# A third fixed order of the steps, with its lags and PSUM banks, for a delta-rule attention, softmax attention and mixture-of-experts kernel on one core

## The reference

```
x = x + delta_rule_block(layernorm(x))
x = x + transformer_block(layernorm(x))

delta_rule_block:   q, k, v = silu(causal_conv4(x @ Wq / Wk / Wv)), 16 heads of 64; rope(q), rope(k), both normalised
                    beta = sigmoid(x @ bw + bb);  alpha = exp(-exp(A_log) * softplus(x @ gkw + gkb + dt_bias))
                    per token: o = q S + D (q.k) v;  S = alpha (S - beta k (k S)) + beta k v
                    ((x @ Wg) * silu(rmsnorm(o) * onorm_w)) @ Wo
transformer_block:  x + softmax attention (16 heads of 8) on layernorm(x); then a router picks 2 of 8 experts;
                    each expert is gelu(m @ W1[e] + b1[e]) @ W2[e] + b2[e], with 512 hidden features
```

## Time and profile before

| | us |
|---|---|
| median of three runs | 5545.79 |
| lowest and highest run | 5541.89, 5554.14 |
| the profiled execution | 5533.59 |
| its span, first to last instruction | 5531.7 |

### The profile page before, as it was taken

One profiled execution on the slowest core, in us unless ns is written; L12 is line 12 of the kernel. 1 busy time (PEld: TensorE's weight loads), 2 busy tenths in 40 slices (PEclk: granted clock), 3 DMA queues, 4 the chain that ended last, 5 costly groups with the idle time before them and its releaser, 6 DMA issues.

```text
span 5531.7 us, 111231 instructions
## 1 busy us (share of the span) xinstructions
PE 4792.2 (87%) x40448; PEld 3609.5 (65%) x40448; DVE 4623.1 (84%) x11457; ACT 3445.0 (62%) x6166; POOL 2085.5 (38%) x1485
## 2 busy tenths in 40 slices
...
GB/s 59 10 11 34 43 43 34 28 32 37 43 43 34 24 32 41 43 33 32 33 33 42 43 33 32 32 34 43 43 34 32 32 34 43 43 34 32 31 34 56
DMA packets 214453, 197.13 MB, mean 36 GB/s; under 512 B 13848, under 2 KB 176416, under 8 KB 209696
## 3 DMA queue, kind: packets, MB, share of 16 engines
...
## 4 chain that ended last, share of the span: by engine, by line
DVE 52%; PE 38%; issue 8%; ACT 1%; SPq 0%; DMA 0%; POOL 0%; DVEq 0%; POOLq 0%; ACTq 0%
PE bank L984 36%; DVE acc L1390 10%; DVE tmpb L1556 6%; DVE NP L1526 6%; DVE Gam L1559 5%; DVE mx L1653 3%; DVE Gam L1512 3%; DVE moe L1738 2%; PE bank L988 2%; DVE QK L1671 1%; DVE QK L1479 1%; DVE Gam L1563 1%; DVE rot L1475 1%; DVE ms L1603 1%; DVE Kt L1543 1%
## 5 line engine op out<-in xcount | busy, mean ns | idle before, releaser
L1390 DVE SCALAR_TENSOR_TENSOR acc<-bank,conv_w,acc 128x255 f32<-128x255 f32 (+2 forms) x2304 | 925.1, 470 | 27.3 <-ACT acc L791 26.4
L717 POOL TENSOR_TENSOR sq<-acc 128x256 f32<-128x256 f32 x256 | 191.2, 747 | 1734.5 <-ACT acc L797 1722.3
L984 PE MATMUL bank<-QK 64*128 64x256 f32 (+1 forms) x4096 | 603.3, 352 | 211.8 <-DVE mx L1653 97.7
L984 PE MATMUL bank<-W,h 128*128 128x128 f32 x4096 | 579.7, 302 | 190.1 <-issue 103.3
L984 PEld LDWEIGHTS bank<-W,h 128*128 128x128 f32 x4096 | 551.7, 215 | 237.1 <-issue 129.6
L984 PE MATMUL bank<-mT,W 128*128 128x256 f32 x2048 | 626.4, 447 | 60.3 <-issue 39.7
L984 PEld LDWEIGHTS bank<-QK 64*128 64x128 f32 (+1 forms) x4096 | 288.6, 142 | 523.7 <-issue 346.0
L966 ACT ACTIVATE h<-bank,b 128x256 f32<-128x256 f32 x1024 | 416.7, 479 | 288.6 <-PE bank L984 286.7
L984 PEld LDWEIGHTS bank<-mT,W 128*128 128x128 f32 x2048 | 420.9, 220 | 219.2 <-issue 155.3
L729 POOL TENSOR_TENSOR rot<-rot,sin 128x512 f32<-128x512 f32 x256 | 337.3, 1317 | 450.8 <-DVE rot L1475 450.8
L1559 DVE TENSOR_TENSOR Gam<-Gam,tmpb 128x31 f32<-128x31 f32 (+15 forms) x992 | 448.1, 452 | 34.1
...
## 6 DMA issues: line engine op xcount, KB each, us to landing
W<-in_W SPq DMA_DIRECT2D x512, 256.0 KB, 3.2
...
```

What stands on the lines that cost most here:

```text
L984: return mm(out_, lhsT, rhs, start=first, stop=last)
L1390: v.scalar_tensor_tensor(acc[:, n % 2, m, j:T], ps[:, m, 0:T - j], conv_w[:, kind, c, PAD - j:KT - j], acc[:, n % 2, m, j:T], ALU.mult, AL ...
```

## The change

All five lists and the bank table are replaced; no step function is changed, and every list holds the same set of steps. Some steps change sides of the point at which a turn is cut, and their lags follow: the lists of the engines begin some nine steps earlier in the cycle, SyncE's largest lag is 4, not 3, so `turns` runs one turn more, in which only SyncE has steps left. Two lines of each table:

```diff
     "sp": """
-        xnG:0@1 x1:0@3 expert:1@3 expert:0@3 expert:2@3 expert:3@3 expert:4@3 expert:5@3 QK1:0@1 store:0@3 expert:7@3
-        expert:6@3 xin:0@0""",
+        expert:6@4 expert:7@4 store:0@4 xnG:0@1 expert:0@3 x1:0@3 expert:1@3 QK1:0@1 expert:2@3 expert:3@3 expert:4@3
+        xin:0@0 expert:5@3""",
...
 BANK = """
-    GT:0=2 KS:0=2 KS:1=6 QS:0=1 QS:1=0 S:0=6 Wo:0=3 alpha:0=0 alpha:1=1 alpha:2=5 alpha:3=7 alpha:4=4 alpha:5=7
+    GT:0=7 KS:0=6 KS:1=3 QS:0=6 QS:1=7 S:0=6 Wo:0=6 alpha:0=3 alpha:1=0 alpha:2=7 alpha:3=5 alpha:4=1 alpha:5=6
```

More of the change, by code:

```diff
@@ L57 @@
[L57 to L58 removed]
+        Dv:1@2 dots:6@1 cos:6@1 QSadd:0@2 QSadd:1@2 dots:7@1 root:0@2 sin:6@1 norm:0@2 rstd:0@0 cos:7@1 root:1@2
+        norm:1@2 sin:7@1 nrm:0@1 frstd:0@2 frstd:1@2 X:0@1 cos:0@0 dots:0@0 sin:0@0 cos:1@0 dots:1@0 sin:1@0 cos:2@0
+        dots:2@0 dots:3@0 vscale:0@1 vscale:1@1 sin:2@0 cos:3@0 sin:3@0 cos:4@0 dots:4@0 sin:4@0 Dv:0@1 dots:5@0 cos:5@0
@@ L59 @@
+        frstd:2@2 sin:5@0 R1:0@1 R1:1@1 xs:0@2""",
     "act": """
[L60 to L68, removed]
@@ L69 @@
-        silu:7@0 low:2@1 square:6@0 ex:0@2 low:3@1 gelu:0@2 gelu:1@2 square:7@0""",
-    "pe": """
[L71 to L77, removed]
-        max:12@2 max:11@2 max:14@2 max:15@2 up:14@3 up:13@3 up:15@3 mrow:1@2 mrow:0@2 mrow:2@2 sums:0@0 st:0@2 down:6@3
-        st:3@2 st:2@2 st:1@2 down:7@3 pv:0@2 st:4@2 mrow:3@2 st:5@2 st:6@2 st:7@2 qk:3@0 st:8@2 st:11@2 st:9@2 pv:1@2
-        st:10@2 st:12@2 sums:1@0 st:13@2 pv:2@2 st:14@2 qk:4@0 sums:2@0 st:15@2 qk:6@0 qk:5@0 pv:3@2 join1:0@1 sums:3@0
-        join1:1@1 ctx:0@2 join2:0@1 join2:1@1 ctx:1@2 top:0@1 ctxT:0@2 top:1@1 cross:0@1 fWo:0@2 cross:1@1 low:0@1
-        sums:4@0 low:1@1 qk:7@0 S:0@1 o:1@1 KS:0@1 KS:1@1 QS:0@1 o:0@1 top:2@1 sums:5@0 top:3@1 cross:2@1 mT:0@2
-        cross:3@1 router:0@2 low:2@1 QS:1@1 low:3@1 up:1@2 up:0@2 o:2@1 o:3@1 alpha:1@0""",
```

77 lines of the change are left out of this document (49 added, 28 removed).

## The result

The changed kernel takes 5247.2 us (median of four runs, 5244.47 to 5256.83). The kernel before took 5543.84 us on the same chip (5531.1 to 5554.14). The ratio is 0.9469, 95% interval 0.9446 to 0.9493: 5.3% faster. I had forecast 5610 us, slower, with 5455 us as the lower end of the range. The sign was wrong and the range did not hold the time.

A forecast was written before the change was run, and what follows sets the result against it. A turn is a TensorE-bound stretch (some 50 us) plus a VectorE-bound one (some 117 us). 4.2-1.9-0.2 = +2.1 us a turn, times 31 = +65 us; 5533.6+65+12 = 5610 us, range 5455 to 5700.

The forecast's parts named there:

- T: The start of `join1:0` on TensorE, right behind `close`, from which the prediction counts times within a turn.
- A: The stretch from T to `o:3`, bound by TensorE: +4.2 us a turn, ends +1.9 and +6.7.
- both `join2` 3.6: TensorE behind `close`: both `join2` matmuls take 3.6 us, so they end at T+12.5.
- my first rival: TensorE's clock comes back earlier, at T+6: -2.9 us a turn in all, 5456 us; chance 0.17.
- The tap wait: VectorE behind `close`: L1390 waits some 7 us a turn for ScalarE's `tap:5`.
- B: VectorE's `solve` steps beside GpSimd: -1.9 us a turn, ends -6.4 and +1.
- come just before `close`: Both `vscale` on GpSimd run among the last short `solve` steps, costing twice 1.7 us a turn.
- my second rival: The ports are free: `vscale` falls wholly beside the transposes, -2.0 us a turn in all, 5484 us; chance 0.20.
- the burst beside maxima: GpSimd's burst runs beside VectorE's `max` reductions, which read PSUM, giving back all 6.4 us a turn.
- the price of a meeting: A `vscale` on GpSimd blocks one `solve` step on VectorE, taken as 1.7 us each.
- C: Other waits and gaps, with 1 us saved and 0.8 for `max:0`: -0.2 us a turn, ends -2 and +2.
- The table load of `ex`: ScalarE: `ex` with its table load (1.28 us) stands before the copy of `top:3`, for which `cross:3` waits.

The follow-up runs named there:

- a_qk6_late: The changed kernel with `qk:6` moved from between `ctx:0` and `ctx:1` to behind `cross:1` on TensorE: 5334.6 us, ratio 0.9641.
- b_region: The kernel before with `ctx:0`, `qk:6`, `ctx:1` behind `join1:0` (`ctx:1` in bank 3) and ScalarE's `upper:0` ahead of `join1:0`: 5551.2 us, ratio 1.0031.
- a_tap5: The changed kernel with ScalarE's `tap:5` moved ahead of the `join2` copies: 5234.2 us, ratio 0.9462.
- a_vscale_early: The changed kernel with `vscale:0` and `vscale:1` moved ahead of `dots:3` on GpSimd: 5379.8 us, ratio 0.9729.
- a_swap1_late: The changed kernel with VectorE's `swap:1` moved from behind `max:10` to behind `solve:12`: 5392.5 us, ratio 0.9761.
- b_vscale_late: The kernel before with `vscale:0` and `vscale:1` moved behind `dots:3` on GpSimd: 5515.0 us, ratio 0.9969.
- b_ctx_qk6b: The kernel before with `ctx:0`, `qk:6`, `ctx:1` moved behind `join1:0` on TensorE, VectorE's `ctx` steps matched, `ctx:1` in bank 3: 5556.7 us, ratio 1.0041.

## Why the prediction was wrong

**What bounds a turn: right.** A stretch from T to `o:3` bound by TensorE and one bound by VectorE; in the turns shown both became shorter, by 2.6 to 6.3 us (T+49.1 and T+52.8 became T+46.5) and by some 5 us.

**A, +4.2 us forecast, of it 2.8 in this stretch; -2.6 to -6.3 measured there.** The failed step is "both `join2` 3.6", with all the durations of the earlier trace rows beside it: I laid the new order end to end at half clock. With the wide `qk:6` right behind `join1:0` the clock was back at T+6, `join2` ended at T+10.2 and not T+12.5, and `KS:0` came at T+27.8 and not T+32.1. That was my first rival, with 0.17. Its condition (back at T+6) came true, and a_qk6_late shows that it hangs on the place of `qk:6`; b_region, where it came true too and nothing was gained, shows that this place is not enough. I had discounted it by a turn in which other wide matmuls did not help. a_qk6_late prices the part at 87/31 = 2.8 us a turn, less than the 5 that I gave. The tap wait was right in place, and roughly in size (5.27 us, forecast 7), and a_tap5 shows that it is almost free, as the text held ("the long wait mostly changes its place"). VectorE's idle time from T to `o:3`, which I had put near 19 us, was 11.8.

**B, -1.9 us forecast, -5.9 on the solve lines measured.** The failed step is that both `vscale` "come just before `close`". `dots:3`, which stands ahead of them, waits for `silu:3`, and that ended at 2708.40 us, 1.2 us after `close` had begun at 2707.17. So the first product ran beside a transpose, the second beside operations that read PSUM, and they cost next to nothing: my second rival, by its own condition. GpSimd and ScalarE there:

```profile
2708.47 0.73 POOL L717 TENSOR_TENSOR sq<-acc 128x256 f32<-128x256 f32 x1 [15.57 <-ACT acc L797]
2709.16 3.77 POOL L711 TENSOR_TENSOR V<-V,nrm 128x1024 f32<-128x1024 f32 x2
```

```profile
2707.77 0.63 ACT L797 ACTIVATE acc<-acc 128x512 f32<-128x512 f32 x1
```

The other half, the burst beside maxima, was right, as was the price of a meeting (twice 1.58 us in a_vscale_early; I had taken 1.7). Unforeseen was that the new order pays 1.7 us of it back on L1479.

**C, -0.2 us.** `max:0` costs 0.4 us a turn (the wait at L1653 is 5.9 us in 16 turns; I took 0.8). The table load of `ex` ended before its input was there in the turn shown; the two added loads were not looked at one by one.

**The rivals were set against each other.** I gave each of them alone a chance and a time, and none to both together, though nothing in my text ties one to the other. Together they read 2.1-5-4.1 = -7.0 us a turn, 5329 us; the measured -9.2 lies beyond even that. The lower end of the range, at one rival's case, left the combination out. And the terms are not a sum: 2.2 us of work put back on VectorE cost 4.9 us a turn (a_swap1_late), while 0.5 us taken from it in the kernel before saved 0.6 (b_vscale_late).

**Still open:** what starts and what ends a half-clock spell, why the second one lasts some 20 and 27 us in the old order (b_ctx_qk6b, b_region) and 10 in the new one, and so how much of the 5.3% is the clock's own. Of the 9.2 us a turn, 4.8 are VectorE's shorter work, which the rows show. The other 4.4 are shorter waits. The place of `qk:6` alone is worth 2.8, with the clock; the rest no single run prices.
